# Graph network on one Trainium2 core: the gather ring is handed on in groups of two tiles instead of four

## The reference, cut to what matters

```python
msg = h[src] * alpha[:, :, None]                           # pass "gat", 4 heads
x1 = segment_sum(msg, dst, n) + gat_bias
logits2 = einsum('ec,ec->e', q[d2], k[s2]) * scale         # pass "attn", 1 head
out = segment_sum(v[s2] * segment_softmax(logits2)[:, None], d2, n)
msg = xs_j * a[:, :, None]                                 # pass "typed", 8 heads, weighted edges
out = segment_sum(msg, dst, n)
```

## Time and profile before

| what | value |
|---|---|
| time, median of 3 runs | 4017.09 us (4016.53 to 4025.2) |
| profiled execution: span of its own instructions (no other time of it is given) | 4831.1 us, 814.0 us over the median |
| busy in it | PE 63%, PEld 45%, DVE 64%, ACT 30%, POOL 56% |
| mean granted TensorE clock | 0.788 |
| gathers of gat | 145.1 to 1432.0 us |
| gathers of attn | 1643.9 to 2924.3 us |
| gathers of typed | 3144.4 to 4388.8 us |

### The profile page before, as it was taken

One profiled execution on the slowest core, in us unless ns is written; L12 is line 12 of the kernel. 1 busy time (PEld: TensorE's weight loads), 2 busy tenths in 40 slices (PEclk: granted clock), 3 DMA queues, 4 the chain that ended last, 5 costly groups with the idle time before them and its releaser, 6 DMA issues. The chain is left out here.

```text
span 4831.1 us, 70737 instructions
## 1 busy us (share of the span) xinstructions
PE 3023.5 (63%) x14389; PEld 2152.2 (45%) x14389; DVE 3082.1 (64%) x9652; ACT 1461.7 (30%) x4590; POOL 2703.3 (56%) x2963
## 2 busy tenths in 40 slices
PE   5344455555557567777777778834555565656998
PEld 4233333333345344444445455523333343434998
DVE  6455666666667545555555556846666777778786
ACT  2222222222225434445545455500001011101333
POOL 3556665555550245666555552565666666653787
PEclk9667777777778877888888888967777777777999
DMA  4544444444432433333333343643444444443221
GB/s 135 150 120 132 132 134 130 131 134 130 127 112 89 131 94 107 111 110 109 104 102 110 104 113 96 209 134 106 121 122 125 117 123 124 120 121 86 68 71 53
DMA packets 290341, 561.56 MB, mean 116 GB/s; under 512 B 85318, under 2 KB 183278, under 8 KB 289998
## 3 DMA queue, kind: packets, MB, share of 16 engines
q0 software_dynamic: 115872, 326.30, 24.3%
q10 hardware_dynamic: 101462, 168.49, 11.4%
q1 hardware_dynamic: 72664, 63.00, 4.5%
HBM read 479.67 MB, written 77.89 MB: 115 GB/s over the span
## 5 line engine op out<-in xcount | busy, mean ns | idle before, releaser
L464 PE MATMUL psum<-big,onehots_or_distances 128*128 128x264 f32 (+2 forms) x5280 | 1889.5, 485 | 314.6 <-issue 143.2
L464 PEld LDWEIGHTS psum<-big,onehots_or_distances 128*128 128x128 f32 x5280 | 1065.1, 233 | 554.9 <-issue 266.0
L278 POOL DMA_INDIRECT big<-table_attn,src_by_edge x782 | 741.1, 948 | 751.2 <-SPq L271 343.3
L668 DVE TENSOR_TENSOR acc<-acc,psum 128x264 f32 (+2 forms) x1320 | 559.4, 424 | 872.7 <-remote 404.2
L278 POOL DMA_INDIRECT big<-table_gat,src_by_edge x782 | 770.3, 985 | 528.0 <-SPq L271 289.1
L278 POOL DMA_INDIRECT big<-table_typed,src_by_edge x782 | 772.9, 988 | 483.0 <-SPq L271 242.4
L427 PE MATMUL psum<-big,onehot_t 128*128 x2640 | 510.4, 308 | 245.1 <-issue 132.8
L447 PE MATMUL psum<-growth,ones 64*128 64x4 f32 (+2 forms) x330 | 89.5, 341 | 901.1 <-DVE growth L610 855.6
L510 DVE SCALAR_TENSOR_TENSOR dot_products<-psum,big 128x258 f32<-128x258 f32 x880 | 364.4, 421 | 421.2 <-PE psum L427 240.8
L645 DVE TENSOR_TENSOR big<-big,psum 128x512 f32<-128x512 f32 x880 | 594.3, 675 | 9.6 <-issue 0.5
L447 PEld LDWEIGHTS psum<-growth,ones 64*128 64x128 f32 (+2 forms) x330 | 74.8, 281 | 980.6 <-DVE growth L610 923.5
(11 more groups left out here) (284 smaller groups left out, 4101.0 us busy)
## 6 DMA issues: line engine op xcount, KB each, us to landing
onehot_t<-onehots ACTq DMA_DIRECT2D x73, 512.0 KB
big<-visit_positions ACTq DMA_DIRECT2D x55, 512.0 KB
onehots<-big ACTq DMA_DIRECT2D x37, 512.0 KB
big<-onehots ACTq DMA_DIRECT2D x37, 512.0 KB
big<-in_x_dram SPq DMA_DIRECT2D x98, 128.0 KB, 2.7
big<-table_gat,src_by_edge POOLq DMA_INDIRECT x782
big<-table_attn,src_by_edge POOLq DMA_INDIRECT x782
big<-table_typed,src_by_edge POOLq DMA_INDIRECT x782
```

Of the source, the lines that this page charges most:

```text
L278: pool.indirect_dma_start(X[:, t % RING, :], None, ph.table, bass.IndirectOffsetOnAxis(ap=m.src[:, t:t + 1], axis=0)).then_inc(S[f"rows{t ...
L464: last = nc.tensor.matmul(sum_ps(w), onehot_at(v), rows, start=(v % 2 == 0), stop=(v % 2 == 1))
L668: nc.vector.tensor_tensor(row, row, sum_ps(w), ALU.add).then_inc(S["added"], 1)
```

## The change

Groups of two tiles instead of four, everywhere: 22 groups of two in the same ring of 44 tiles, 22 `rows` semaphores, 391 turns of SP's loop instead of 196, LAG 18 groups instead of 9 (36 tiles in both), and thresholds for every second visit instead of every fourth, so that a batch's record has 8 places and 8 thresholds. The ring, the number and size of the gathers and the arithmetic stay.

```diff
-QUARTER = 4
+QUARTER = 2
 NTQ = (NT + QUARTER - 1) // QUARTER
...
-LAG = 9
+LAG = 18
 TAIL = 16
 PAIRS = G // 2
-RECORD = PAIRS + 4
+RECORD = PAIRS + G // QUARTER
...
     def needs_of(engine, k):
         at = k * RECORD + PAIRS
-        return nc.values_load_multi_w_load_instructions(m.index[32:33, at:at + 4], engines=[engine], min_val=1, max_val=NT)[1]
+        return nc.values_load_multi_w_load_instructions(m.index[32:33, at:at + G // QUARTER], engines=[engine], min_val=1, max_val=NT)[1]
...
-            sp.dma_start(records[:, :, PAIRS:RECORD], dram.by_quarter[NV // 2:NV // 2 + VISIT_END // 4].rearrange("(a k g) -> a k g", a=1, g=4)).then_inc(S["end"], 16)
-            sp.dma_start(m.index[64:65, 0:NV // 4], dram.by_quarter[3 * NV // 4:NV].rearrange("(a n) -> a n", a=1)).then_inc(S["end"], 16)
+            sp.dma_start(records[:, :, PAIRS:RECORD], dram.by_quarter[2 * NV // QUARTER:2 * NV // QUARTER + VISIT_END // QUARTER].rearrange("(a k g) -> a k g", a=1, g=G // QUARTER)).then_inc(S["end"], 16)
+            sp.dma_start(m.index[64:65, 0:NV // QUARTER], dram.by_quarter[3 * NV // QUARTER:4 * NV // QUARTER].rearrange("(a n) -> a n", a=1)).then_inc(S["end"], 16)
...
-        dram.by_quarter = dr("quarter_places", [NV], I32)
+        dram.by_quarter = dr("quarter_places", [4 * NV // QUARTER], I32)
```

## The result

The change makes the kernel slower: 4065.91 us (4060.61 to 4073.79, 4 runs) against 4018.64 us for the kernel before (4 runs), a ratio of 1.0113 with a 95% interval of 1.0100 to 1.0125. The forecast was 4052 us, slower.

The account below looks back on a forecast made before the run. POOL's issuing of gathers was taken to bound all three passes. PE's thresholds +44, the ring's first turn -5, landing -5 and setup +1 make +35 us on 4017, so 4052 us, with a range of 3992 to 4105.

Parts of the forecast that it names:

- What bounds the kernel: All three passes: POOL's issuing of gathers bounds the timed runs; DVE's pauses of 663.8 us mostly belong to the profiled execution.
- PE's thresholds: PE in attn: 220 more threshold chains, 88 us if all exposed, half taken: +44 us, bounds 0 and 121.
- no change: Rival: POOL paces attn as well and PE's longer queue hides in its wait for rows; 4012 us, chance 0.22.
- A gather therefore costs POOL 1.25 us: POOL, every pass: 0.946 us a gather plus 0.30 us idle, so 782 gathers need at least 977.5 us.
- the 65 us: POOL's idle time in all three passes of a timed run, about what better handing on can win.
- faster: Rival: finer handing on gives back two thirds of POOL's idle 65 us in gat and typed, -40 us; 3977 us, chance 0.20.
- Landing: SP's freeing behind landed groups: POOL's slack grows from 6.25 to 8.75 us; -5 us, ends 0 and -65.
- The ring's first turn: POOL's wait for the first free place in each pass gets shorter; -5 us over three passes, ends 0 and -36.
- SP, POOL, ACT, setup: SP's doubled turns, POOL's added waits and ACT's doubled thresholds cost 0; setup and semaphores +1 us.
- The clock falls: Rival: more gaps on PE in attn lower its granted clock from 0.83 to 0.75, +97 us; 4149 us, chance 0.08.
- The sum: Whole kernel: 44 - 5 - 5 + 1 = +35 us, carried to the median as 4052 us.

Follow-up runs that it names:

- before_again: The kernel before, unchanged, profiled a second time: 4025.38 us in this execution, span 4023.5 us.
- e3: The kernel before, but PE in attn loads its threshold at every second visit, the same one twice: 4068.17 us, ratio 1.0104.
- e2: The changed kernel, but PE in attn loads a threshold at every fourth visit again: 4032.04 us, ratio 1.0022 to the kernel before.
- e5: The kernel before, with DVE's comparison L633 reading one operand from PSUM instead of SBUF: 3976.34 us, ratio 0.9880.
- e6: The changed kernel with PE's thresholds at every fourth visit and L633 reading one operand from PSUM: 3933.18 us, ratio 0.9773 to the kernel before.
- e9: e5 (groups of four, L633 from PSUM) with LAG 8 instead of 9: 3939.90 us, ratio 0.9798 to the kernel before.
- e4: The changed kernel with L633 reading one operand from PSUM instead of SBUF: 3976.88 us, ratio 0.9882 to the kernel before.

## Why the prediction was right or wrong, point by point

**What bounds the kernel: right.** The pauses were taken for an accident of one execution, and before_again has none of them; POOL's issuing paces the passes, attn too (its gathers take 980.7 us in before_again, the floor). PE was the engine to watch in attn, as e3 shows, but not at 93%: that figure comes from the first execution with its clock of 0.83, and in before_again PE is busy for 719.84 of 870 us there, 83%, at 0.97.

**PE's thresholds: right in mechanism, and in size partly by luck.** Forecast +44 us, half of the 88 us that full exposure would make; alone they cost +44.4 us (e3), and taking them out of the change gives 39.1 us back (e2), the same within the spread of the runs. The price of a load, 305 ns, held. But of the two reasons for the half, the lower clock was hardly there in before_again and after (0.97 and 1.00 in attn's middle), and the wait for the scans is 13.1 us in before_again instead of 61.4. What shrank instead was PE's waits for rows, from 93.2 to 49.9 us: the wait that the rival "no change" had named. These 43 us are about what was not paid of the 88. By the floor of about 600 ns that the Trainium skill has (DMA: Bandwidth & Descriptors, section Latency and other measured facts), the term would have been 1.6 x 44 = 70 us, an estimate; neither run shows as much.

**"A gather therefore costs POOL 1.25 us", and with it the 65 us of idle time: the step that failed, though the forecast came out.** 1.25 us is the floor, and it is what attn pays. In gat and typed L633 holds up gathers for 41 and 39 us in before_again, and it was these 80 us, not waiting, that made most of the 95 us by which the three passes' gathers are over the floor. The 65 us, on which the rival "faster" was priced, were therefore mostly not idle time: the price of a gather was read from single rows, and the maximum of 1427 and 1446 ns that stands in the earlier trace rows for gat and typed, against 1102 for attn, was not followed up. It didn't spoil the sum, because the change touches this term by little: +12.4 us in typed, through more collisions.

**Landing: right in mechanism, its size hidden.** Forecast -5 us with ends 0 and -65. In the change gat moved by -2.9 us; POOL's waits for `freed` in gat, 13.9 us and up to 1.9 us long in before_again, are down to gaps of 0.3 us in after, but its collisions grew by 10 us. With the collisions away the term is worth 43 us (e5 to e6), and some 36 of them can be had by LAG alone (e9). The slack of 6.25 us was read rightly; how often a group lands later than that was not, and SP's waits do not tell it, since a wait of SP counts from its last step and not from a gather's start.

**The ring's first turn: nothing.** The -5 us came from waits of the first execution; all of before_again has only 13.9 us in 20 waits, the longest 1.9 us, so there was nothing like 26.06 us to win.

**SP, POOL, ACT, setup: right.** SP's 1107 loads are there at the price of the earlier trace rows (median 267 ns), and no run shows a cost of them; POOL's gathers with a wait have no longer gap; with the collisions away typed takes 978 us with ACT's 8 thresholds and with 4. Setup moved by 0.7 us where 1 was forecast.

```profile
L266 SPq TENSOR_LOAD <-index x1107: 260/267/1576, 194.7 to 3632.3; - x185
```

**The rivals.** "No change" fell with e3, though half of its mechanism was at work (above). "The clock falls" fell by the windows of attn, 1480 to 2350 us (busy us of PE, PEld, DVE, ACT and POOL, then the granted clock, DMA share and GB/s), before_again and then after:

```profile
1480.00:2350.00 870.00, 719.84 (x4072) 490.55 (x4071) 629.74 (x2707) 562.65 (x1702) 658.88 (x693) 0.97 0.51 140
```

```profile
1480.00:2350.00 870.00, 691.81 (x3908) 456.12 (x3907) 613.23 (x2604) 536.55 (x1629) 639.89 (x674) 1.00 0.48 136
```

PE has less to do in a microsecond, and the granted clock doesn't go down: 1.00 against 0.97, the level of 2.4 GHz nearly throughout. The rule on brief idle times in the Trainium skill (TensorE: Matmul & The Clock Gate, section A second HAM failure mode), which the forecast put beside that rival, is not seen at work here, with 220 more loads between the matmuls. "Faster" was a real mechanism covered by two others: finer handing on with the larger slack is worth some 40 us, once PE's chains and L633's hold are out of the way.

**The sum.** Forecast 44 - 5 - 5 + 1 = +35 us; by pass, the spans show +38.2 in attn, +12.4 in typed, -2.9 in gat and +0.7 before it, +48.4. The medians are 4065.91 - 4018.64 = 47.3 us apart. The forecast's +35 us fell short of the spans' +48.4 by 12.4 us of collisions in typed that it didn't have and by 10 us of gains of which 2.9 came, less 6 us in attn (38.2 for 44). So it was near because its one large term was near.

## What to carry to other kernels

Added register loads cost nothing here on SP and ACT, which wait most of the time, and 0.20 us a chain on PE in attn, which comes to set the pace: before one doubles the thresholds, look at whether the engine that loads them is near the bound. A gather whose maximum is half above its median in some stages and not in others deserves the question what runs beside it; here a comparison with both operands in SBUF was the answer, and moving one operand to PSUM is worth 45 to 97 us (e5 against before, e6 against e2), with DVE's comparison as long as before (680 against 682 ns). A gain that seems to be nothing may be covered by another bound: after the cover is taken away, measure the term again, and try whether a plain constant (here LAG) gives the same.

## What had not been expected of the hardware

That a single DVE instruction of 680 ns holds up an indirect gather on POOL by up to 0.6 us (1582 ns where the median is 949), and that the same instruction with one operand from PSUM does not: the longest gather of gat and typed falls from 1582 and 1472 ns in after to 1117 ns in e4, the level of attn. And that one profiled execution can hold 664 us of pauses that a second one doesn't show and that the timed runs, 814 us shorter, have no room for.
